# Attention: the order in which a pass issues its entries, differences, score units and sums

## The reference

```python
scores = jnp.einsum('bhqd,bhkd->bhqk', q, k) * scale
scores = jnp.where(causal[None, None], scores, -jnp.inf)
att = jax.nn.softmax(scores, axis=-1)
y = jnp.einsum('bhqk,bhkd->bhqd', att, v)
y = y.transpose(0, 2, 1, 3).reshape(b, t, c)
return y @ Wc
```

## Time and profile before

| | us |
|---|---|
| median of 3 runs (1885.11 to 1886.77) | 1885.85 |
| the profiled execution | 1885.63 |
| its span, first to last instruction | 1883.9 |

### The profile page before, as it was taken

How to read it: one execution, slowest core, us unless ns; L and a number is a source line. 1 busy time by engine, 2 the same in 40 slices (tenths; PEclk the granted TensorE clock), 3 DMA queues, 4 the chain that set the end, 5 groups by cost and what they waited for, 6 DMA issues and landing times.

```text
span 1883.9 us, 41858 instructions
## 1 busy us (share of the span) xinstructions
PE 1820.1 (97%) x13875; PEld 681.7 (36%) x13875; DVE 1670.1 (89%) x4759; ACT 1591.1 (84%) x1924; POOL 536.8 (28%) x647
## 2 busy tenths in 40 slices
PE   6999999999789999999999999999999999999998
PEld 3556555555322323233232323323232322323223
DVE  5899999999789999999999999999999999999961
ACT  4676676675169999999999999999999999999994
POOL 1121121121244141523414152441415144141220
PEclk8999999999769999999999999999999999999999
DMA  5232333335422314041431414143141414324112
GB/s 185 68 106 84 90 104 89 89 100 123 103 63 46 58 24 65 22 73 25 78 54 49 65 45 84 32 83 53 50 65 45 79 35 84 53 50 65 36 36 81
DMA packets 160324, 129.01 MB, mean 68 GB/s; under 512 B 95344, under 2 KB 144752, under 8 KB 159768
## 3 DMA queue, kind: packets, MB, share of 16 engines
q1 hardware_dynamic: 159064, 126.84, 31.2%
q10 hardware_dynamic: 1088, 0.03, 0.0%
HBM read 74.60 MB, written 42.98 MB: 62 GB/s over the span
## 4 chain that ended last, share of the span: by engine, by line
PE 43%; ACT 15%; issue 8%; DVE 5%; DMA 1%; POOL 1%; SPq 1%; DVEq 0%; ACTq 0%; POOLq 0%
PE pv L1749 16%; ACT prob L1529 13%; PE sm L1711 10%; PE st L1734 10%; PE sm L1682 3%; PE st L1721 2%; DVE sm L1610 2%; ACT excess L1522 1%; DVE sm L1598 1%; PE sm L1675 1%; DVE pm L1615 1%; DMA scratch_i<-inverse 1%; DVE pm L1598 1%; DVE pm L1610 1%; ACT Y L1512 0%
## 5 line engine op out<-in xcount | busy, mean ns | idle before, releaser
L1529 ACT ACTIVATE prob<-st 128x1024 f32<-128x1024 f32 x1088 | 1048.1, 1028 | 53.6 <-PE st L1734 43.6
L1749 PE MATMUL pv<-prob,V 128*32 128x512 f32 (+3 forms) x5120 | 586.4, 539 | 0.3 <-ACT Y L1512 0.2
L1598 DVE CUSTOM_DVE_ANT_0 sm<-sm,mask 128x256 f32<-128x256 f32 (+3 forms) x1024 | 473.4, 520 | 32.0 <-PE sm L1711 27.3
L1711 PE MATMUL sm<-K,Q 48*128 48x512 f16 (+3 forms) x2112 | 479.7, 348 | 13.2 <-DVE pm L1598 5.5
L1734 PE MATMUL st<-Q,K 50*128 50x512 f16 (+3 forms) x2560 | 478.5, 352 | 9.8 <-ACT prob L1529 6.0
L1615 DVE TENSOR_REDUCE pm<-sm 128x1 f32<-128x512 f32 x640 | 412.0, 683 | 39.9 <-PE sm L1711 36.6
L1488 POOL TENSOR_SCALAR_AFFINE_SELECT prob<-prob 128x256 f32<-128x256 f32 (+1 forms) x448 | 191.4, 442 | 869.6 <-ACT prob L1529 860.5
L1610 DVE CUSTOM_DVE_ANT_0 sm<-sm,excess 128x512 f32<-128x512 f32 x448 | 301.2, 711 | 17.9 <-PE sm L1711 17.3
L1711 PEld LDWEIGHTS sm<-K,Q 48*128 48x128 f16 x2112 | 151.9, 95 | 327.9 <-DVE pm L1610 115.0
L1734 PEld LDWEIGHTS st<-Q,K 50*128 50x128 f16 x2560 | 125.7, 93 | 363.1 <-ACT prob L1529 265.2
L1522 ACT ACTIVATE excess<-st 128x1024 f32<-128x1024 f32 x218 | 220.4, 1024 | 8.7 <-DVE pm L1615 5.1
(11 more groups left out here) (201 smaller groups left out, 1899.4 us busy)
## 6 DMA issues: line engine op xcount, KB each, us to landing
Q<-scratch_q SPq DMA_DIRECT2D x102, 128.0 KB, 4.3
K<-scratch_k SPq DMA_DIRECT2D x102, 128.0 KB, 7.1
x<-in_x SPq DMA_DIRECT2D x16, 512.0 KB, 4.4
scratch_v<-Rt SPq DMA_DIRECT2D x64, 128.0 KB, 2.0
scratch_r<-Rt SPq DMA_DIRECT2D x16, 512.0 KB, 3.2
V_raw<-scratch_v SPq DMA_DIRECT2D x16, 512.0 KB, 10.1
Yc<-Y SPq DMA_DIRECT2D x124, 64.0 KB
spread<-scratch_i SPq DMA_DIRECT2D x124, 64.0 KB, 2.2
```

What stands on the lines that cost most here:

```text
L1529: act.activation(prob_of(quad, k)[:, :, :], st[number % ST][:, :, :], ACT.Exp).then_inc(exp_done, 1)
L1598: i = dve.tensor_tensor_reduce(x, x, mask[:, CH - block_width(t, k):], 1.0, -3e38, ALU.add, ALU.max, best(h, t, k))
L1711: i = pe.matmul(dst[:, at:at + width], lhsT=Q[slot][r, h // 2, t * P:(t + 1) * P], rhs=K[slot][r, h // 2, k * CH:k * CH + width], start=Tr ...
L1749: i = pe.matmul(pv[2 * DH * h:2 * DH * (h + 1), CH - width:CH], lhsT=V[quad % VSLOTS][:, j, h, :], rhs=prob_of(quad, u)[:, h % 2, at:at + ...
```

## The change

The table is written anew with the same letters: 115 `m`, 68 `s`, 14 `x`, 36 `w`. The steps of each kind keep their own order, and all numbers of buffers stay. No other line differs.

```diff
 TIMETABLE = (
-    "wsmmswxmmwmsmsmmsmmswmmsmxwxmmsmwmxmsmmsmmsmwsmmsmwsmmsmwmxmxmmsmmxw"
-    "msmsmwsmmmxmswsmmsmsmmsmwmsmsmwmmsmswsmmmswxmmswsmmsmwsmmsmwsmsmmxwm"
-    "smmswmsmmswsmmmswxmwmssmmwsmsmmmswsmmswsmmmswsmmswsmmmswsmmswsmsmmms"
-    "wxmmmswsmmswmsmmxwmsmmswxmmms"
+    "mwsmmsmwxmmsmxmmwsmxmwsmmmswsmmmsmsmxmwmsmmswmmsmswxmmmswsmmxmxmsmmm"
+    "swmssmmwsmmmswsmmsmxmwmssmmwmmsmswsmmmswsmmswmxmmxwsmmsmsmwsmmsmwmsm"
+    "smwmmxsmwsmmmswsmwmmssmwmsmsmmswsmmmswsmmswsmmmswsmmswsmmmswxmsmmmsw"
+    "smmsmwsmmswmsmmxwsmsmmmxwmsms"
 )
```

## The result

The new order is slower: 1893.38 us, median of 6 runs (1892.74 to 1895.29), against 1886.0 (1885.11 to 1886.77) of the kernel before in 6 runs of its own. The ratio is 1.0041 (95% interval 1.0031 to 1.0051). The forecast was 1878.3 us, inside 1862 to 1899, with a chance of 0.24 on slower.

The account below looks back on a forecast made before the run. No engine was taken to bound the kernel; ACT lost time at gaps holding sums steps or project entries. Loss falling from 5.47 to 4.98 us saves 0.49 per pass, 7.3 over 15: 1885.6 - 7.3 = 1878.3 us, range 1862 to 1899.

Parts of the forecast that it names:

- a bare `w` just fits: At a wide sums step with no entry beside it, PE's 1.8 us fits within ACT's 1.84 us of work.
- four dear gaps: Gaps of before with an entry ahead of `w`, after a gap of two entries: together 1.36 us, mean 0.34.
- the two read as free: Gaps of before with an entry ahead of `w`, after one or no entry: nothing lost, mean -0.015 us.
- The price list: ACT's loss per kind of gap, from one pass of before, applied to the new table: 4.98 against 5.47 us.
- Five gaps with an entry ahead: New table, tokens 1, 21, 75, 126, 144, after one or no entry: -0.015 us each, -0.08 in all.
- The `p`: Four project entries of the new table, all alone: 0.017 us each, 0.07 per pass.
- two-sided ones: Four new gaps with entries on both sides of `w`: 0.61 us for one, 0.26 for the others, 1.38 in all.
- The base: ACT's loss in one pass of the kernel before, summed by kind of gap: 5.47 us.
- Costed at nothing: Mask waits (bound 0 to 0.4 us a pass), the close `excess` buffer (at most 0.71) and Q rows: no cost.
- Rival 2: Slower, 1899 us: eight new gaps with an entry ahead of `w` cost 0.17 us each, not nothing; chance 0.18.
- Rival 1: No change, 1885.6 us: each of 36 `w` and 4 `p` loses 0.14 us whatever stands beside it; chance 0.18.
- Rival 3: More gain, 1864 us: DVE's work is smoother, so `w` after three entries costs as little as others; chance 0.14.

Follow-up runs that it names:

- both others light: ACT's and DVE's operations cut to 64 columns, all matmuls kept: 1794.0 us in the kernel before's order, 1795.15 us in the new order.
- DVE light: Only DVE's operations cut to 64 columns: 1868.75 us in the kernel before's order, 1872.4 us in the new order.
- the four mixes: New order in tokens 0 to 61, 62 to 106, 107 to 157 or 158 to 232 alone, old elsewhere: 1898.7, 1896.5, 1905.2, 1904.0 us.
- ACT light: Only ACT's operations cut to 64 columns: 1863.2 us in the kernel before's order, 1869.9 us in the new order.
- the third order: Another table of the same steps, drawn to shorten PE's and ACT's stretches between sums steps, replacing the kernel before's: 1888.74 us, ratio 1.0007.

## Why the prediction was wrong, point by point

**What bounds the kernel** held: no engine does, ACT needs 77.4 us, the pass loses 5.2 more, in gaps that hold a sums step or a `p` (the 46 others lose nothing, -0.2 and -0.1 in all before and after). It missed that PE needs 77.5 us itself. It had set 24 us of weight loads against 81.5 of busy matmuls and leaned to a room of 5.3 us. With both others light PE still has 24 us of weight loads, and the pass takes 77.5: busy matmuls were the nearer measure. The Trainium skill ("Perfetto Trace Analysis", Identifying the Most-Contended Engine) would judge TensorE's room by weight-load busy time, beside the share of peak FLOPs, and not by matmul busy time. Of the two this case's trace speaks for matmul busy time, and the measurement decides.

**The step that failed** is the cause given for a gap's loss: "a bare `w` just fits", 1.8 us against 2 x 0.92 = 1.84, and "entries do that when their bank of `sm` is not yet read by DVE". The unit ahead of the sums step can't begin when ACT begins the unit two before it; it must wait for that activation's end, 1.02 us, and 0.06. Of three units' 2.76 us this leaves 1.68 for what the prediction rightly added up to 1.80: over three units a bare `w` loses 0.12 (after three entries 0.14 was measured, and read as DVE's doing), and an entry that begins a pair of its own 0.33, with DVE light or not. This loop is at nearly every wide sums step: the unit ahead starts 0.05 to 0.15 us after its tile comes free at 30 of 32 before and at 31 of 32 after. Whether a gap shows the loss depends on what ACT has already lost between the same three units. So the price did not belong to "after two entries". Two of the four dear gaps lose 0.43; the other two, each one sums step behind one of these, lose 0.13 and 0.17. And the two read as free (tokens 73 and 161) have a loss of 0.37 and a copy between their three units.

**The price list** fails where that matters. Five gaps with an entry ahead were priced at -0.08 on two gaps of before: 0.46, nearly all of it in the gap of token 126 (0.41), which stands behind a stretch of three units, so that no sums step lies between its three; the other four have one there and lose 0.05. The `p` were priced on one gap: 0.31 for 0.07. `w` alone costs 0.39 more than its two prices. The two-sided ones were priced too dear, as the text said they might be (0.89 for 1.38).

**The base.** 5.47 was read along one pass; ten give 5.42 for the same kinds of gap, so the choice of the pass cost 0.05. The 46 other gaps were put at nothing on both sides: -0.20 before and -0.08 after, another 0.12 the wrong way.

**Costed at nothing.** PE's weight loads wait for POOL's masks 14.1 us over the run instead of 7.0, 0.35 us a pass more in the 13 passes, within the bound given; how much of it reaches the end was not tried. They also wait 25.1 us for the copies of `pv` instead of 9.3, which no text had priced; but the four gaps where a chunk's first sums step stands lose less than before (0.24 for 0.87). The close buffer of `excess` and the Q rows show no loss. The last pass, put within 1 us of nothing, with its neighbour adds 2.0, of which a neighbour like the 13 passes is 0.45.

**Rivals.** Rival 2 had the outcome's side and, at token 126, its place; but its eight gaps together cost 0.89 where 0.70 was priced, so most of the 0.66 lies elsewhere, in bare `w` (0.39) and `p` (0.24). Its condition ("if the bank is not free there") was not the one at token 126: the bank was free, the tile of `st` was not. That the outcome fell on its side was luck. Rival 1, a fixed loss for each `w` and `p`, falls with the four mixes: the same steps took 10 to 19 us more. Rival 3 falls too: the nine gaps after three entries lose 0.16 each, not 0.04.

**Open.** Why the whole new order is 7 us slower rather than 0 or 15 can't be read from any single place: with DVE light, with ACT light and in the whole kernel its passes are about as much slower, and no account here forecasts 0.3 us of a pass.

## What to carry to other kernels

Before you price an order, make the engines light in turn: here three runs show that PE and ACT need the same time and that the rest is what the buffers between them and DVE cost. Count a buffer's loop from the *start* of the operation that frees it to the start of the one that needs it, latency included; here two tiles give less than two operations' worth of time. A price by neighbours, from two or three cases in one pass, did not carry to a new order, and the third order, drawn by a rule, found what the rule leaves out.

## What the runs showed of the hardware that I had not expected

Half-array matmuls cost PE by the pair. Two on different halves of its rows run side by side in 0.21 us, and an odd one ahead of a sums step costs the same 0.21: 1.755 us with six, 1.967 with seven, and +0.213 for the seventh put in by hand. An eighth is nearly free where the pair was begun (0.03 and 0.05 us at tokens 104 and 204, given back in the next stretch). The Trainium skill ("TensorEngine Tiling (Array Packing)", Key Properties) says that different tiles of the array can work in parallel. The trace agrees, and adds the price of the odd one.
